# A fused decoder layer: how the row maxima are spread, a chain of loops written out, transposes for the maxima's row, and a rearranged end of the experts' part

## The chip, the cores and the metric

The kernel runs on one core of a Trainium2 chip. TensorE (PE in the profile) multiplies matrices, with PEld as its weight loads; VectorE is DVE, ScalarE is ACT, GpSimd is POOL, SyncE is SP. The metric is the device time of one launch in microseconds (us), the median of the runs.

## The reference

One decoder layer over 1024 tokens of width 128, in three parts, each followed by a layer norm: a Mamba2 pair (forward and backward), attention of the 1024 tokens to a context of 6404 rows plus the tokens themselves (8 heads of 128), and a mixture of 8 experts (each token goes to 2) with a shared expert. Cut to what the change touches:

```python
# attention: q from the layer's rows x, keys and values from [context, x]
sim = einsum('bhid,bhjd->bhij', q * DH ** -0.5, k)
out = einsum('bhij,bhjd->bhid', softmax(sim, axis=-1), v)     # then @ Wo + bo, residual, layer norm
# experts
topv, topi = top_k(softmax(xn @ router_w), 2); topv = topv / sum(topv)
out = sum over e of comb[:, e] * (silu(clip(gate_e, -10, 10)) * up_e) @ down_w[e]
out = out + shared expert
y = layernorm(x + out)
```

## The kernel before

**Attention** is 16 blocks (`NBLK`) of 512 query columns. A block runs through the keys in `NS` = 30 steps of two chunks of 128 keys: 7 head steps, a loop of 3 turns of 6 steps (`LOOP0`, `LOOPN`), 5 tail steps from `TAIL`. All operands are pairs of fp16 numbers (high and low part), so a chunk takes three products with A (scores) and three with the weights P (values), each 512 columns wide. In a step PE computes the scores, ACT takes the exponential twice (L1030 to fp16, L1033 to fp32), DVE subtracts for the low part (L1470), and PE multiplies with the values two steps later.

Meanwhile block b-1 finds the maxima of block b: 60 **units**, one PE product each into one of two banks of PSUM, read by a DVE maximum (L1438). PE may compute unit n only when unit n-2 has been read. `UNITS_HEAD` and `UNITS_TURN` say how many units stand in each step; three units stand in a step as one behind the first chunk's scores, one behind the second's, one between the two halves of the values; two units leave out the middle one. In its order DVE does a step's maxima first and then its low part. At the tail `max_to_row` turns the four columns of maxima into a row, DVE puts it into A (`max_row`), `project` multiplies the block before with the output matrix, and `a_side` computes A of the block after the next. From block 6 on `a_side` works by tile: 24 products of 128 columns, where before it takes 6 of 512. Blocks 0, 14 and 15 are written out; PE runs blocks 1 to 5, 6 to 8 and 9 to 13 in three loops with a register for the block's number.

Block 15 finishes tile 7 of the tokens (`LAST_TILE`). Tiles 0 to 6 (`FRONT`) are normalised, routed and sent to their slots during block 15.

**Experts** are 31 units of work in the order `ORDER`: 21 slots of 128 rows (13 of them with the expert's number in a register), the two halves of the shared expert, 8 experts on tile 7. For a unit PE computes gate and up, DVE clips the gate (`clip`, L1758), ACT takes silu (L1107), DVE multiplies (`hidden`, L1767), ACT casts to the high part (L1114), POOL or DVE subtracts the low part (L814, L1781), and PE multiplies down three units later. DVE runs `side_work` between them: norm, transposition and routing of tile 7. At the end the slots' rows come back from DRAM (`yt`), two per token, DVE adds them to `acc`, and the last norm goes to `xf` and by eight stores of one tile to the output.

The order of all work on an engine is the order of its code; between engines stand semaphores. A chain of norm pieces (`tile_norm`) waits after nearly every instruction (`settle`). The inverse root is computed with shifts and three Newton steps in it (L1510 to L1517).

## Time and profile before

| | us |
|---|---|
| median of 3 runs | 1765.81 (1763.61 to 1766.6) |
| the profiled execution's own time | 1766.59 |
| its span, first to last instruction | 1764.8 |
| PE busy | 1698.3 (96%) |
| DVE busy | 1450.4 (82%) |
| ACT busy | 1087.9 (62%) |
| POOL busy | 272.3 (15%) |

The profile is of one execution. A PE product's record is longer than the distance to the next one, since products overlap: the start times tell how fast they follow each other. The attention blocks lie between about 171 and 1665 us, the experts between 1666 and 1750 us, the last norm and the stores behind that.

### The profile page before, as it was taken

What the parts mean: (1) busy time and instruction counts of PE and PEld (TensorE: products, weight loads), DVE (VectorE), ACT (ScalarE), POOL (GpSimd) and SP (SyncE); (2) the same over time, 40 slices, a digit from 0 to 9 for tenths busy, and PEclk for the clock granted to TensorE, in tenths of its full rate; (3) what the DMA queues carried; (4) which work ended last, traced back from release to release, by engine and by line L of the source; (5) the groups of instructions that cost most, each with busy time, mean ns of one, the idle gap of its engine ahead of it and who ended that gap; (6) DMA issues with size and microseconds to landing.
All of it is one profiled execution on the core that took longest, in us unless ns stands there. A gap on an engine that the chain in (4) does not pass through costs nothing.

```text
span 1764.8 us, 31344 instructions
## 1 busy us (share of the span) xinstructions
PE 1698.3 (96%) x9273; PEld 860.6 (49%) x9273; DVE 1450.4 (82%) x2318; ACT 1087.9 (62%) x1333; POOL 272.3 (15%) x356
## 2 busy tenths in 40 slices
PE   6978999999999999999999999999999999999996
PEld 4855444444444444444444444444444444444585
DVE  7958988888888879797878888888879797877667
ACT  4555666666666666666666666666666666567663
POOL 4745993000000000000000000000000000001363
PEclk8989999999999999999999999999999999999998
DMA  5001110000000000000000000000000000000101
GB/s 179 2 1 37 55 55 4 0 0 0 0 0 0 0 0 0 0 0 0 0 0 0 0 1 0 0 0 0 0 0 0 0 0 0 1 0 1 54 25 43
DMA packets 20669, 20.24 MB, mean 11 GB/s; under 512 B 6735, under 2 KB 18259, under 8 KB 20230
## 3 DMA queue, kind: packets, MB, share of 16 engines
q1 hardware_dynamic: 19494, 17.20, 3.2%
q0 software_dynamic: 1120, 2.31, 0.4%
q8 instruction: 34, 0.56, 0.1%
q14 instruction: 21, 0.17, 0.0%
HBM read 15.27 MB, written 4.23 MB: 11 GB/s over the span
## 4 chain that ended last, share of the span: by engine, by line
PE 88%; DVE 5%; issue 3%; ACT 2%; POOL 0%; DMA 0%; DVEq 0%; ACTq 0%; POOLq 0%
PE PS L1875 88%; ACT p_arena L1040 1%; DVE mxs L1438 1%; DVE mxs L1719 1%; ACT p_arena L1033 1%; DVE w_arena L1219 0%; DVE z_arena L1767 0%; DVE w_arena L1393 0%; DMA w_arena<-in_x 0%; ACT z_arena L876 0%; POOL p_arena L814 0%; DVE w_arena L1207 0%; DVE m_arena L1520 0%; DVE p_arena L1470 0%; DVE m_arena L1399 0%
## 5 line engine op out<-in xcount | busy, mean ns | idle before, releaser
L1030 ACT ACTIVATE p_arena<-PS 128x1024 f16<-128x1024 f32 (+1 forms) x480 | 484.4, 1009 | 523.5 <-PE PS L1875 523.3
L1875 PE MATMUL PS<-a_arena,z_arena 128*128 (+1 forms) x2832 | 746.6, 380 | 1.5 <-DVE a_arena L1734 1.4
L1875 PE MATMUL PS<-p_arena,z_arena 128*128 128x512 f16 x2800 | 740.6, 379 | 1.4 <-ACT p_arena L1040 0.3
L1470 DVE TENSOR_TENSOR p_arena<-p_arena 128x1024 f16<-128x1024 f32 (+1 forms) x480 | 574.2, 1196 | 100.5 <-ACT p_arena L1033 90.2
L1438 DVE TENSOR_REDUCE mxs<-PS 128x512 f32 (+1 forms) x900 | 581.8, 667 | 86.6 <-PE PS L1875 83.2
L1033 ACT ACTIVATE p_arena<-PS 128x1024 f32<-128x1024 f32 (+1 forms) x480 | 482.0, 1004 | 0.0
L1875 PEld LDWEIGHTS PS<-a_arena,z_arena 128*128 (+1 forms) x2832 | 274.1, 98 | 326.8 <-issue 2.0
L1875 PEld LDWEIGHTS PS<-p_arena,z_arena 128*128 128x128 f16 (+1 forms) x2800 | 269.3, 98 | 311.8 <-ACT p_arena L1040 8.8
L1875 PE MATMUL PS<-z_arena,a_arena 128*128 (+3 forms) x1024 | 353.4, 360 | 10.4 <-DVE mxs L1438 8.1
L785 POOL IOTA r_arena<- 128x16 f32 x1 | 0.1, 145 | 1296.4 <-DVE acc L1484 1296.4
L1875 PEld LDWEIGHTS PS<-z_arena,a_arena 128*128 (+1 forms) x1024 | 97.8, 98 | 143.7 <-DVE mxs L1438 26.2
L1875 PE MATMUL PS<-w_arena 128*128 128x64 f32 (+5 forms) x268 | 40.3, 293 | 6.6 <-DVE w_arena L1219 3.9
L1719 DVE TENSOR_REDUCE mxs<-PS 128x2 f32<-128x1024 f32 (+1 forms) x30 | 34.1, 1184 | 10.9 <-PE PS L1875 10.8
L712 POOL TENSOR_SCALAR p_arena<-p_arena,mv,rs 128x127 f32<-128x127 f32 x50 | 41.8, 847 | 0.0
L1875 PE MATMUL PS<-z_arena,w_arena 128*128 128x128 f16 x504 | 37.9, 221 | 2.9 <-DVE z_arena L1767 1.6
L774 POOL TENSOR_SCALAR w_arena<-w_arena 128x256 f32<-128x256 f32 (+1 forms) x50 | 40.3, 806 | 0.0
L1758 DVE TENSOR_SCALAR z_arena<-PS 128x512 f32<-128x512 f32 x31 | 21.4, 690 | 23.0 <-PE PS L1875 16.1
L778 POOL TENSOR_TENSOR w_arena<-w_arena 128x256 f16<-128x256 f32 (+1 forms) x50 | 37.7, 754 | 4.2
L1875 PEld LDWEIGHTS PS<-VO,p_arena 128*128 128x128 f32 x256 | 33.4, 191 | 4.3
L1107 ACT ACTIVATE z_arena<-z_arena 128x512 f32<-128x512 f32 x31 | 19.5, 630 | 25.9 <-DVE z_arena L1758 25.9
L1875 PEld LDWEIGHTS PS<-z_arena,w_arena 128*128 (+1 forms) x504 | 31.6, 97 | 7.4 <-issue 3.3
L1020 ACT ACTIVATE a_arena<-PS 128x512 f32 (+1 forms) x32 | 19.1, 597 | 25.8 <-PE PS L1875 25.7
(323 smaller groups left out, 1019.4 us busy)
## 6 DMA issues: line engine op xcount, KB each, us to landing
w_arena<-in_L_ffn_gate_up_w SPq DMA_DIRECT2D x8, 512.0 KB, 3.6
p_arena<-in_ctx SPq DMA_DIRECT2D x2, 1600.0 KB, 9.1
w_arena<-in_L_ffn_down_w SPq DMA_DIRECT2D x8, 256.0 KB, 3.9
a_arena<-in_L_xattn_Wkv SPq DMA_DIRECT2D x1, 1024.0 KB, 5.7
a_arena<-xg_dram SPq DMA_DIRECT2D x12, 65.0 KB, 2.0
xg_dram<-VO SPq DMA_DIRECT2D x1, 715.0 KB, 7.4
xg_dram<-VO SPq DMA_DIRECT2D x1, 650.0 KB, 8.9
w_arena<-in_x SPq DMA_DIRECT2D x1, 512.0 KB, 4.3
```

Of the source, the lines that this page charges most:

```text
L712: g.tensor_scalar(ctx_sb[:, c, 1:P], ctx_sb[:, c, 1:P], mv[:, c, 0:1], rs[:, 3, c:c + 1], ALU.subtract, ALU.mult).then_inc(z_scaled, 1)
L774: g.tensor_scalar(src, src, WS, 0.0, ALU.mult, ALU.add).then_inc(w_scaled, 1)
L778: g.tensor_tensor(lo, src, hi, ALU.subtract).then_inc(stage_used, 1)
L1020: s.activation(A[:, b % 4, 2 * g, :], PS[:, 7 - g, :], ACT.Copy, scale=1 / AHS).then_inc(a_hi, 1)
L1030: s.activation(Phi[:, r % 3, 0:w], ps, ACT.Exp, scale=1 / SSC).then_inc(hi_ready, 1)
L1033: s.activation(P32[:, r % 2, 0:w], ps, ACT.Exp, scale=1 / SSC).then_inc(p32_ready, 1)
L1107: s.activation(sil[:, u % RING], gcl[:, u % RING], ACT.Silu, scale=1 / (XS * WS)).then_inc(f_silu, 1)
L1438: v.tensor_reduce(mxs[:, i, bass.ds(kb, 1)], PS[:, 6 + par, 0:w], AX.X, ALU.max).then_inc(mx_read, 1)
L1470: v.tensor_tensor(Plo[:, r % 3, at:w], P32[:, r % 2, at:w], Phi[:, r % 3, at:w], ALU.subtract).then_inc(lo_ready, 1)
L1719: v.tensor_reduce(mxs[:, i:i + 2, kb:kb + 1], PS[:, pair % 2 * 2:pair % 2 * 2 + 2, 0:w], AX.X, ALU.max).then_inc(mx_read, 2)
L1758: v.tensor_scalar(gcl[:, u % RING], PS[:, u % 2], lim, -lim, ALU.min, ALU.max).then_inc(f_clip, 1)
L1875: return t.matmul(o, l, r, start=start, stop=stop)
```

## The change

1. `UNITS_TURN` goes from 3, 3, 3, 3, 2, 2 to 2, 3, 3, 3, 3, 2 units per step of a loop turn.
2. `max_to_row` uses four transposes where four fp32 products with the identity stood.
3. PE's blocks 6 to 13 are written out, each with its numbers as constants; the loop over the turns inside a block stays.
4. Behind block 15 the evacuation `U_sb` is split between ACT and DVE, and the clip of unit 0 stands ahead of `project_acc`. PE waits for one semaphore more.
5. The norm of tile 7 goes one piece per unit, from unit 2 to 8 (`NORM0`), its transposition from step 5 to 10, its routing from step 10 to 15.
6. At the end POOL adds the slots' rows of tiles 0 to 3 and DVE those of tiles 4 to 6, ahead of the last low part; one chain of roots serves all 8 tiles; DVE writes rows of tiles 7 to 2, POOL of 0 and 1; three stores (tiles 5 to 7, 0 to 1, 2 to 4).

```diff
-UNITS_TURN = [3, 3, 3, 3, 2, 2]
+UNITS_TURN = [2, 3, 3, 3, 3, 2]
...
+NORM0, TURNED, ROUTED = 2, 10, 15
...
-    put(5, 1, "turned", 1, 0)
-    put(10, 1, "routed", 1, 0)
+    put(TURNED, 1, "turned", 1, 0)
+    put(ROUTED, 1, "routed", 1, 0)
...
-            for c in range(TC):
-                sp.wait_ge(fin, c + 1)
-                sp.dma_start(outr[:, c, :], xf[:, c, :]).then_inc(stored, 16)
-            sp.wait_ge(stored, 16 * TC)
+            sp.wait_ge(fin, 3)
+            sp.dma_start(outr[:, 5:TC, :], xf[:, 5:TC, :]).then_inc(stored, 16)
+            sp.wait_ge(base_rows, TC + 2)
+            sp.dma_start(outr[:, 0:2, :], xf[:, 0:2, :]).then_inc(stored, 16)
+            sp.wait_ge(fin, 6)
+            sp.dma_start(outr[:, 2:5, :], xf[:, 2:5, :]).then_inc(stored, 16)
+            sp.wait_ge(stored, 48)
...
+            def rows_added(part):
+
+                r = Y_TILES[part]
+                rows = acc[:, r.start:r.stop]
+                pool.wait_ge(yt_ld[part], 16)
+                for k in range(2):
+                    g.tensor_tensor(rows, rows, yt[:, r.start:r.stop, k], ALU.add).then_inc(half_acc, 1)
+                    pool.wait_ge(half_acc, k + 1)
...
+            pool.wait_ge(dn_acc, BY_DVE[number("shared", 1, NF - 1 - HT)])
+            rows_added(0)
+            pool.wait_ge(out_roots, 1)
+            for t in range(2):
+                norm_rows(xf[:, t, :], acc[:, t, :], t, t).then_inc(base_rows, 1)
...
-            evac(NBLK - 1)
+            act.wait_ge(pv_done, NS * NBLK)
+            act.wait_ge(o_ps, 2 * (NBLK - 1))
+            s.copy(U_sb[:, 0], PS[:, 4, :]).then_inc(u_evac, 1)
...
+            dve.wait_ge(pv_done, NS * NBLK)
+            v.tensor_copy(U_sb[:, 1], PS[:, 5, :]).then_inc(o_half, 1)
+            clip(0)
...
+            def front_added():
+
+                r = Y_TILES[1]
+                rows = acc[:, r.start:r.stop]
+                dve.wait_ge(dn_acc, BY_DVE[number("shared", 1, NF - 1 - HT)])
+                dve.wait_ge(yt_ld[1], 16)
+                for k in range(2):
+                    settle(v.tensor_tensor(rows, rows, yt[:, r.start:r.stop, k], ALU.add))
+
+            def out_stats(tiles):
+
+                for t in tiles:
+                    last = v.bn_stats(st6[:, t, :], acc[:, t, :])
+                return last
...
-                if u == 0:
-                    dve.wait_ge(o_acc, 2 * NBLK)
-                    tile_norm([LAST_TILE], 2 * NF, 0)
-                    tile_norm([LAST_TILE], 2 * NF, 1)
-                elif u in (1, 2):
-                    tile_norm([LAST_TILE], 2 * NF, 2 * u)
-                    tile_norm([LAST_TILE], 2 * NF, 2 * u + 1)
-                elif u == 3:
-                    tile_norm([LAST_TILE], 2 * NF, 6)
-                elif u == 7:
+                if NORM0 <= u < NORM0 + 7:
+                    if u == NORM0:
+                        dve.wait_ge(o_acc, 2 * NBLK)
+                    tile_norm([LAST_TILE], 2 * NF, u - NORM0)
...
             for u in range(NUNITS):
-                clip(u)
                 if u:
+                    clip(u)
...
             hidden(LAST_UNIT)
+            front_added()
             low_dve(LAST_UNIT)
             for u in range(NUNITS, NUNITS + 6):
                 for kind, a, t in work_at(u - 1, 0) + work_at(u - 1, 1):
                     small_dve(kind, a, t)
-            front_done(0)
-            front_done(1)
-            front_done(2)
-            front_done(3)
+            out_stats(Y_TILES[1])
+            dve.wait_ge(half_acc, 2)
+            out_stats(Y_TILES[0])
             dve.wait_ge(dn_acc, BY_DVE[-1])
             dve.wait_ge(last_ps, 1)
             added(LAST_TILE, LAST_BANK, cb[:, E - 1:E]).then_inc(dn_acc, 1)
             dve.wait_ge(dn_acc, BY_DVE[-1] + 1)
-            for piece in range(4, 9):
-                front_done(piece)
-            tile_norm([LAST_TILE], 2 * NF, 0, twice=False)
-            tile_norm([LAST_TILE], 2 * NF, 1, twice=False)
-            for piece in range(2, 7):
-                tile_norm([LAST_TILE], 2 * NF, piece, twice=False)
+            settle(out_stats([LAST_TILE]))
+            for piece in range(1, 6):
+                tile_norm(range(TC), 0, piece, twice=False)
+            dve.wait_ge(out_roots, 1)
+            for t in OUT_ROWS:
+                out_row(t, t).then_inc(fin, 1)
...
-                    last = mm(PS[0:1, row_bank(b), i * P:(i + 1) * P], mcol[:, 1, i:i + 1], I32[:])
+                    last = t.transpose(PS[0:1, row_bank(b), i * P:(i + 1) * P], mcol[:, 1, i:i + 1], I32[:])
...
-            with pe.Fori(H - 2, H + 1) as j:
-                block_pe(j, a_by_tile=True)
-            with pe.Fori(H + 1, NBLK - 2) as j:
-                block_pe(j, a_by_tile=True, by_tile=True)
+            for j in range(H - 2, NBLK - 2):
+                block_pe(j, a_by_tile=True, by_tile=j > H)
...
+                    pe.wait_ge(o_half, 2 * (NBLK - 1 - H) + 1)
```

How the change moves instructions, at three places. In these rows a name in brackets is the semaphore waited for.

On PE, the end of a block from 9 to 13, from the last values products ahead of `a_side` (`ah_arena` holds its left operand) on. Before:

```order
L1875 MATMUL PS<-p_arena,z_arena 128x512
L2366 REGISTER_ALU
L1875 ISA [waits o_acc]
L1875 ISA
L1875 MATMUL PS<-z_arena,ah_arena 128x128
L1875 ISA
L1875 MATMUL PS<-z_arena,ah_arena 128x128
```

and now:

```order
L1897 MATMUL PS<-p_arena,z_arena 128x512
L1897 MATMUL PS<-z_arena,ah_arena 128x128 [waits o_acc]
L1897 MATMUL PS<-z_arena,ah_arena 128x128 x23
L1897 MATMUL PS<-a_arena,z_arena 128x512 [waits p32_ready]
L1897 MATMUL PS<-a_arena,z_arena 128x512 x5
```

The 24 products stood among instructions that form their addresses in registers, one at each one or two products; now they stand alone.

On DVE, the first units of the experts (`gcl`, `sil` and `hid` lie in `z_arena`; L1758 is a clip, L1767 a `hidden`). Before:

```order
L1750 TENSOR_TENSOR a_arena<-a_arena,r_arena 128x21 [waits dve_step]
L1758 TENSOR_SCALAR z_arena<-PS 128x512 [waits f_gate]
L1499 BN_STATS st<-acc 128x6 [waits o_acc]
L1503 BN_AGGR mv<-st 128x2 [waits dve_step]
L1505 TENSOR_SCALAR rs<-mv 128x1 [waits dve_step]
L1507 TENSOR_SCALAR rs<-mv 128x1
L1758 TENSOR_SCALAR z_arena<-PS 128x512 [waits f_gate,dve_step]
L1767 SCALAR_TENSOR_TENSOR z_arena<-PS,z_arena 128x512 [waits f_up,f_silu]
```

and now (L1745 is the clip, L1795 `hidden`):

```order
L1778 COPY p_arena<-PS 128x512 [waits pv_done]
L1745 TENSOR_SCALAR z_arena<-PS 128x512 [waits f_gate]
L1498 RECIPROCAL rden<-PS 128x2 [waits o_ps]
L1505 SCALAR_TENSOR_TENSOR acc<-PS,rden,acc 128x128 [waits o_rd]
L1505 SCALAR_TENSOR_TENSOR acc<-PS,rden,acc 128x128 [waits o_half]
```

The clip of unit 0 passed `project_acc` and the slots' destinations, and the norm's pieces stand behind unit 1's `hidden`.

On DVE, the end, behind the last two `hidden`. Before:

```order
L1781 TENSOR_TENSOR p_arena<-z_arena,p_arena 128x512 [waits dn_ps,f_hi]
L1772 SCALAR_TENSOR_TENSOR acc<-PS,wt_arena,acc 128x128 [waits dn_acc,dn_ps] x3
L1814 TENSOR_TENSOR acc<-acc,z_arena 128x512 [waits yt_ld0,dn_acc]
L1816 TENSOR_TENSOR acc<-acc,z_arena 128x512 [waits half_acc]
L1814 TENSOR_TENSOR acc<-acc,z_arena 128x384 [waits yt_ld1]
L1816 TENSOR_TENSOR acc<-acc,z_arena 128x384 [waits half_acc]
L1499 BN_STATS st<-acc 128x6 [waits half_acc]
```

and now:

```order
L1841 TENSOR_TENSOR acc<-acc,z_arena 128x384 [waits yt_ld1,dn_acc]
L1841 TENSOR_TENSOR acc<-acc,z_arena 128x384 [waits dve_step]
L1809 TENSOR_TENSOR p_arena<-z_arena,p_arena 128x512 [waits dn_ps,f_hi,dve_step]
L1800 SCALAR_TENSOR_TENSOR acc<-PS,wt_arena,acc 128x128 [waits dn_acc,dn_ps] x3
L1846 BN_STATS st<-acc 128x6 x3
L1846 BN_STATS st<-acc 128x6 [waits half_acc]
```

Two adds went to POOL (waited for by `half_acc`), the other two passed the last low part.

## Rows read from the trace of the kernel before

**Rows 1.** Busy time by stretch: start:end, length, each engine's busy time, PEclk, DMA

```profile
642.50:736.10 93.60, 93.08 (x447) 43.17 (x446) 79.23 (x106) 59.38 (x65) 0.00 (x0) 1.00 0.00 0
1020.40:1115.20 94.80, 94.20 (x465) 44.23 (x464) 79.42 (x106) 59.38 (x65) 0.00 (x0) 1.00 0.00 1
1494.50:1586.70 92.20, 91.69 (x438) 42.47 (x437) 77.33 (x106) 58.21 (x63) 1.85 (x14) 1.00 0.00 1
1586.70:1663.00 76.30, 75.95 (x390) 37.62 (x388) 54.13 (x131) 55.05 (x60) 23.61 (x21) 1.00 0.07 19
```

**Rows 2.** Timeline of block 13's tail on PE: start, length, engine, line, operation

```profile
1471.43 1.46 PE L1875 MATMUL PS<-p_arena,z_arena 128*128 128x512 f16 x6
1472.73 1.46 PE L1875 MATMUL PS<-a_arena,z_arena 128*128 x6
1474.12 1.03 PE L1875 MATMUL PS<-I,mcol 128*1 128x128 f32 x8
1475.08 1.47 PE L1875 MATMUL PS<-p_arena,z_arena 128*128 128x512 f16 x6
```

**Rows 3.** Timeline of PE in block 15, seven fp32 transposes

```profile
1595.74 0.94 PE L2225 MATMUL PS<-I,m_arena 128*128 128x128 f32 x7
1596.51 1.46 PE L1875 MATMUL PS<-a_arena,z_arena 128*128 128x512 f16 x6
```

**Rows 4.** Timeline of PE around `a_side` of block 13, then in the experts

```profile
1482.06 1.46 PE L1875 MATMUL PS<-p_arena,z_arena 128*128 128x512 f16 x6
1483.60 2.35 PE L1875 MATMUL PS<-z_arena,ah_arena 128*128 x24
1485.84 1.47 PE L1875 MATMUL PS<-a_arena,z_arena 128*128 x6
...
1739.14 1.50 PE L1875 MATMUL PS<-wt_arena,w_arena 128*128 128x128 f16 x24
1740.48 0.83 PE L1875 MATMUL PS<-w_arena,p_arena 128*128 128x128 f16 x12
```

**Rows 5.** Timeline of block 13's first turn; brackets: idle before, releaser

```profile
1414.27 1.03 PE L1875 MATMUL PS<-p_arena,z_arena 128*128 128x512 f16 x4
1415.00 1.97 DVE L1438 TENSOR_REDUCE mxs<-PS 128x512 f32 x3
1415.74 0.39 PE L1875 MATMUL PS<-z_arena,a_arena 128*128 x1 [0.44 <-DVE mxs L1438]
```

**Rows 6.** DMA of instructions over the span: packets, MB, share

```profile
q8 instruction: 34, 0.56, 0.1%
```

**Rows 7.** Timeline of PE in the first units of the experts

```profile
1671.29 0.83 PE L1875 MATMUL PS<-z_arena,w_arena 128*128 128x128 f16 x12 [0.48 <-DVE z_arena L1758]
1673.19 1.59 PE L1875 MATMUL PS<-z_arena,w_arena 128*128 128x128 f16 x24 [1.07 <-DVE z_arena L1767]
1676.51 1.09 PE L1875 MATMUL PS<-z_arena,w_arena 128*128 128x128 f16 x12 [0.58 <-DVE z_arena L1767]
```

**Rows 8.** Timeline of POOL and DVE there, then DVE's small steps at the end

```profile
1673.87 1.16 POOL L814 TENSOR_TENSOR p_arena<-z_arena,p_arena 128x512 f16<-128x512 f32 x1 [16.78 <-ACT p_arena L1114]
1673.91 1.13 DVE L1517 SCALAR_TENSOR_TENSOR wt_arena<-rs,wt_arena 128x2 f32<-128x2 f32 x1
...
1757.22 0.17 DVE L1514 TENSOR_TENSOR rs<-wt_arena 128x7 f32<-128x7 f32 x1
```

**Rows 9.** Timeline of DVE at the end, and the stores (count, KB each, us to landing)

```profile
1750.35 0.68 DVE L1814 TENSOR_TENSOR acc<-acc,z_arena 128x512 f32<-128x512 f32 x1
1752.85 1.45 DVE L1499 BATCH_NORM_STATS2 st<-acc 128x6 f32<-128x128 f32 x7
1757.83 1.88 DVE L1520 TENSOR_SCALAR m_arena<-acc,mv,rs 128x128 f32<-128x128 f32 x7
1762.53 0.34 DVE L1520 TENSOR_SCALAR m_arena<-acc,mv,rs 128x128 f32<-128x128 f32 x1
out<-m_arena SPq DMA_DIRECT2D x8, 64.0 KB, 1.6
```

More of the change, by code:

```diff
@@ L577, in layer @@
         LAST_BANK = LAST_UNIT % 2
+        OUT_ROWS = range(TC - 1, 1, -1)
         Y_TILES = [range(0, 4), range(4, NF)]
@@ L814, in _ @@
                     g.tensor_tensor(lo, hid[:, u % RING], hi, ALU.subtract).then_inc(f_lo, 1)
-                if u == 5:
+                if u == TURNED:
                     pool.wait_ge(xf_ready, 2)
@@ L1143, in _ @@
                         rows_turned_act(k)
-                if u == 6:
+                if u == TURNED + 1:
                     half_act(1, 0)
-                elif u == 15:
+                elif u == ROUTED + 5:
                     half_act(1, 1)
@@ L1482, in project_acc @@
                         last.then_inc(o_half, 1)
-                        dve.wait_ge(o_half, 2 * (b - H) + k + 1)
+                        dve.wait_ge(o_half, 2 * (b - H) + k + (2 if isinstance(b, int) and b == NBLK - 1 else 1))
                     last = v.scalar_tensor_tensor(out=acc[:, t, :], in0=o[:, i, 0:D], scalar=rden[:, 2 * k + i:2 * k + i + 1],
@@ L1488, in _, with out_row @@
             MAGIC = float(0x5F3759DF)
+            def out_row(t, at):
+                return v.tensor_scalar(xf[:, t, :], acc[:, t, :], mv[:, t, 0:1], rs[:, 3, at:at + 1], ALU.subtract, ALU.mult)
             def tile_norm(tiles, at, piece, twice=True):
@@ L1516, in tile_norm @@
                     dst = rs[:, 3, cols] if piece == 5 else y
-                    settle(v.scalar_tensor_tensor(out=dst, in0=rs[:, 1, cols], scalar=1.5, in1=y, op0=ALU.add, op1=ALU.mult))
+                    last = v.scalar_tensor_tensor(out=dst, in0=rs[:, 1, cols], scalar=1.5, in1=y, op0=ALU.add, op1=ALU.mult)
+                    if piece == 5 and not twice:
+                        last.then_inc(out_roots, 1)
+                    else:
+                        settle(last)
                 else:
                     for k, t in enumerate(tiles):
-                        last = v.tensor_scalar(xf[:, t, :], acc[:, t, :], mv[:, t, 0:1], rs[:, 3, at + w - n + k:at + w - n + k + 1],
-                                               ALU.subtract, ALU.mult)
-                        if not twice:
-                            last.then_inc(fin, 1)
-                    if twice:
-                        last.then_inc(xf_ready, 1)
+                        last = out_row(t, at + w - n + k)
+                    last.then_inc(xf_ready, 1)
             def turned(cols, bank):
@@ L1712, in block_dve, with clip @@
                         a_low(j + 2)
+            def clip(u):
+                dve.wait_ge(f_gate, u + 1)
+                if u >= RING:
+                    dve.wait_ge(f_silu, u + 1 - RING)
+                lim = 10.0 * XS * WS
+                v.tensor_scalar(gcl[:, u % RING], PS[:, u % 2], lim, -lim, ALU.min, ALU.max).then_inc(f_clip, 1)
             for pair in range(NU // 2):
@@ L1750, in _ @@
             v.tensor_tensor(posd, xg_f[:, :, D], unused, ALU.add).then_inc(dest_ready, 1)
-            def clip(u):
-                dve.wait_ge(f_gate, u + 1)
-                if u >= RING:
-                    dve.wait_ge(f_silu, u + 1 - RING)
-                lim = 10.0 * XS * WS
-                v.tensor_scalar(gcl[:, u % RING], PS[:, u % 2], lim, -lim, ALU.min, ALU.max).then_inc(f_clip, 1)
             def hidden(u):
@@ L1804, in small_dve @@
                     v.memset(ui[:, 0:1], 0.0).then_inc(dn_acc, 1)
-            def front_done(piece):
-                if piece < 2:
-                    if piece == 0:
-                        dve.wait_ge(dn_acc, BY_DVE[number("shared", 1, NF - 1 - HT)])
-                    r = Y_TILES[piece]
-                    dve.wait_ge(yt_ld[piece], 16)
-                    rows = acc[:, r.start:r.stop]
-                    v.tensor_tensor(rows, rows, yt[:, r.start:r.stop, 0], ALU.add).then_inc(half_acc, 1)
-                    dve.wait_ge(half_acc, 2 * piece + 1)
-                    v.tensor_tensor(rows, rows, yt[:, r.start:r.stop, 1], ALU.add).then_inc(half_acc, 1)
-                else:
-                    if piece == 2:
-                        dve.wait_ge(half_acc, 4)
-                    tile_norm(FRONT, 0, piece - 2, twice=False)
@@ L1834, in side_work @@
+            def out_stats(tiles):
+                for t in tiles:
+                    last = v.bn_stats(st6[:, t, :], acc[:, t, :])
+                return last
+            def side_work(u):
+                if NORM0 <= u < NORM0 + 7:
+                    if u == NORM0:
+                        dve.wait_ge(o_acc, 2 * NBLK)
+                    tile_norm([LAST_TILE], 2 * NF, u - NORM0)
+                elif u == TURNED + 2:
                     turned_low(1)
-                elif 12 <= u < 15:
-                    route(1, u - 12)
-                elif 17 <= u < 21:
-                    route(1, u - 14)
+                elif ROUTED + 2 <= u < ROUTED + 5:
+                    route(1, u - ROUTED - 2)
+                elif ROUTED + 7 <= u < ROUTED + 11:
+                    route(1, u - ROUTED - 4)
```

2 lines of the change are left out of this document (1 added, 1 removed).

## The prediction, made before the changed kernel had run

> **What bounds the kernel now.** I read busy time by stretch first, then the timeline of one attention block, then that of the last 100 us. In an attention block PE is the bound: 94.20 of 94.80 us busy at a granted clock of 1.00, with DVE at 79.42 and ACT at 59.38 [rows 1]. Products of 512 columns follow each other every 0.216 us: six start at 1471.43 and the next six at 1472.73, 1.30 us apart [rows 2]. So a microsecond less on PE in a block is a microsecond less in the time, unless DVE or ACT then comes late; DVE has 15 us of room per block. What is not 512 columns wide, or waits, is what the change can take. The experts are a chain through PE, DVE, ACT and POOL while it fills, then PE's. Behind 1750 us there is only DVE, in steps of 0.2 us, and the stores.
>
> **Maxima's row.** In `max_to_row` the four fp32 products (eight records) start at 1474.12 and the next ones at 1475.08: 0.96 us [rows 2]. Seven fp32 transposes of the same 128 columns take from 1595.74 to 1596.51, 0.77 us, so 0.11 each and 0.44 for four [rows 3]. Nothing covers them on PE: 0.52 less per block. Blocks 0 to 14 have maxima: 15 x 0.52 = 7.8 us. Bounds: the transposes of rows 3 load 128 columns of weights and these load one, so they may be quicker (all 0.96 gone: 14.4), or no quicker than now (0). I take the nearest row, 7.8. DVE's `max_row` is released 0.5 us sooner, which costs nothing.
>
> The row says 0.44 for four transposes. The Trainium skill, TensorE: Matmul & The Clock Gate, section Terms, calls the transpose mode four times faster for fp32; by that four would take 0.24 and the term would be 10.8. In its Part 4: PE-mode transpose it says that transposes do not count as PE-busy for the clock the way products do, which would speak against this edit; the stretch that holds the seven of rows 3 was at 1.00 throughout [rows 1].
>
> **Blocks written out.** In block 13 `a_side` comes behind six products from 1482.06, which are through at 1483.36; it starts at 1483.60 and lasts until 1485.84, together 2.48 us, or 0.093 per product [rows 4]. 24 products of the same shape with constant addresses, in the experts, take from 1739.14 to 1740.48: 1.34 us, 0.056 each [rows 4]. The difference is the address work in registers, an instruction at each one or two products. 1.14 us less, in blocks 6 to 13: 9.1 us. A second way to it: blocks with six wide products instead take 93.60 where these take 94.80 [rows 1], 1.2 us more, though 24 x 0.056 is about what six wide ones need. Bounds: 0, if the pace is that of weights of this operand; 10 if other address work in these blocks costs something too. I take 9.1. Against it stands the fetching of more code: instructions are 34 packets, 0.56 MB, in all [rows 6], and PE's code grows by half. Block 14 is already written out with the same loop inside, and takes 92.20 [rows 1], which is 94.80 less the `a_side` of 2.48 that it lacks (92.32). So written-out code as such costs nothing there.
>
> **Units per step.** In the first turn, first step, PE has four values products from 1414.27, through at 1415.13, and should compute the step's third unit. It starts at 1415.74: 0.61 us late, since DVE was still at the low part and began the step's first maximum only at 1415.00 [rows 5]. The step before is short (one chunk's values), so PE had run ahead of DVE there. With two units in that step the third does not stand there; PE goes on with the last two values products. In the next step, now of three, DVE has read one maximum fewer (1.97 / 3 = 0.66), and finds itself 0.66 earlier relative to PE, which is more than the 0.61 it was late. The three-unit steps are four in a row as before, and a turn still has 16, so the later steps repeat what they were. One place per block, 15 blocks: 9.1 us. Bounds: 0, if the stall only moves a step; below that, -3, if the three-unit step that now stands one place nearer the tail makes `max_column` late by 0.2. It has room there: the row's products start 0.09 us behind the scores, through at 1474.03, so they hardly wait [rows 2]. I take 9.1.
>
> **Start of the experts.** PE's idle spells ahead of the first products that wait for DVE add up to 0.48 + 1.07 + 0.58 = 2.13 us [rows 7]. They come from clip 0, which waits behind `project_acc`, and then from the pieces of tile 7's norm, one of which lasts 1.13 us instead of 0.16 [rows 8]. The clip of unit 0 now waits for its product alone, which takes the 0.48; the first `hidden` gains less, since unit 1's clip ahead of it stays behind the same `project_acc`. The norm's pieces are gone until unit 2. I take 2.0 of the 2.13. DVE's copy of half of `U_sb` lies beside ACT's and ends before PE asks. Bounds: 3.5, if the later units' shorter waits go too; -1, if pieces in units 4 to 8 meet POOL's low parts and hold up a clip or a low part. The later routing (steps 15 to 25) still ends ahead of the first dense unit's add, so I cost it at nothing; if it were late, the add waits on DVE with the next clips queued behind it.
>
> **The end.** DVE adds from 1750.35 to 1752.85 (2.50), writes the first row at 1757.83, seven rows in 1.88 (0.27 each), and then goes once more through everything for tile 7 until 1762.87; the store lands 1.6 later [rows 9]. Now: the adds leave this path (-2.5), tile 7's statistics join (+0.4, one row more in each of two steps). That gives roots at 1755.7. Against it: POOL and DVE get in each other's way. A DVE instruction of two columns with two operands in SBUF, started 0.04 behind a POOL pass of 1.16, lasted 1.13 and ended with it, where such a step takes 0.17 [rows 8]. DVE's two adds and the last low part have two operands in SBUF, and POOL's last low part and two adds of 512 run just then. Two such waits of 1 us: roots at 1757.7, about where they were. Six rows of 0.27 then end at 1759.3 instead of 1762.9. POOL's two rows, at most 1.16 each, end at 1760.0, and the third store waits for the second: issued at 1760.2 instead of 1762.9. That is 2.7 less; without the waits 4.7; with both adds and the low part each held up twice, 0.7. I take 2.7.
>
> The Trainium skill, SBUF — State Buffer, section Who interferes with whom, has the same as a lock: a DVE instruction with two SBUF inputs and a GpSimd one that reads SBUF exclude each other, whichever starts first. By that rule, the trace agrees.
>
> **The sum.** 7.8 + 9.1 + 9.1 + 2.0 + 2.7 = 30.7. The profiled execution took 1766.59 (its span is 1764.8, 1.8 less), so 1735.9; the median of the runs is 0.8 below it: 1735.
>
> **Rivals.** (a) The stall moves: the unit that waits is another one, and the change of `UNITS_TURN` gives nothing. For it: DVE is as full as before in three-unit steps, where 1.97 of PE's 15 x 0.216 = 3.24 go to the maxima and most of the rest to the low part [rows 2, 5]. Against it: the walk above. 1744. (b) `a_side` keeps its pace, for each product loads new weights. For it: its operand is another one than the experts'. Against it: same shape, same count at 0.056. 1744. (c) Transposes with one column of weights take 0.24: 1732. (d) Slower: code. Each written-out block enters its loop of turns at a new address, and if PE must wait there for its instructions, that comes once or more per block. From 3.8 us per block (30.7 / 8) it cancels all the rest; at 5 us per block the time is 1735 + 40 = 1775. For it: PE's code grows by half, and no row shows a long run of written-out blocks. Against it: block 14 [rows 1]. (e) The clock falls to its lower level of 1.2 GHz behind the transposes: one step of 2.6 us at half the pace in 15 blocks is 39 us more, 1774; against it the 1.00 of the stretch with seven of them.
>
> **Chances.** Forecast 0.70, with a range of its own of 1730 to 1741; (a) 0.10; (b) 0.07; (c) 0.05; (d) 0.03; (e) 0.01; the edits do next to nothing together 0.04. I count as no change what lies within 0.2% (3.5 us), about what a measurement of this kernel can tell. Faster: 0.70 + 0.10 + 0.07 + 0.05 = 0.92; same 0.03; slower 0.05, with (d), (e) and a quarter of the rest. The range reaches from (c) with a better end, 1728, to (a) or (b) with a worse start and end, 1748.
>
> **What would show it.** In the changed kernel's trace: four records of transposes with 0.44 us to the next product; the 24 products of `a_side` within 1.34 us and no gap ahead; no idle spell behind L1438 at the first step of a turn; blocks 6 to 13 at 92.5 us, blocks 1 to 5 at the same; PE's idle spells in the first 15 us of the experts under 1 us; DVE steps of over 1 us while POOL adds; the last row's end at 1759 less the 28 us gained ahead. Blocks that shrink by less than 1.5 us would make the prediction wrong, and a block with a new idle spell at its loop's entry would show (d).

## The result and the profile after

The changed kernel takes 1740.11 us (median of 4 runs, 1737.27 to 1740.54), the kernel before in the same comparison 1765.56 (4 runs): a ratio of 0.9853, 95% interval 0.984 to 0.9865, 25.5 us less. It is faster, and the time lies within the range and 5 us above the 1735 forecast. The profiled execution took 1739.8, its span 1737.8; before they were 1766.59 and 1764.8. The sum of the prediction said 30.7 less, the spans say 27.0. The sections below find the missing 3.7, which is what several larger misses leave when they are added up.

First the busy time by stretch, for the counterparts of [rows 1] (start:end, length, busy us and instructions of PE, PEld, DVE, ACT, POOL, then PEclk and the DMA's share and rate):

```profile
618.40:711.20 92.80, 92.72 (x444) 42.88 (x443) 78.95 (x107) 59.39 (x63) 0.00 (x0) 1.00 0.00 0
1082.60:1175.50 92.90, 92.82 (x462) 43.71 (x461) 79.19 (x107) 59.39 (x63) 0.00 (x0) 1.00 0.00 0
1564.40:1640.70 76.30, 75.95 (x390) 37.62 (x389) 54.18 (x131) 55.05 (x60) 23.62 (x21) 1.00 0.07 19
```

A block with wide `a_side` went from 93.60 to 92.8, one by tiles from 94.80 to 92.9; the prediction had 92.5 for both. The last block is as long as before. The granted clock is 1.00, the 2.4 GHz level, with four transposes in each block. PE's timeline in block 13, counterpart of [rows 2] and [rows 4] (start, length, engine, line, operation):

```profile
1453.03 1.46 PE L1897 MATMUL PS<-a_arena,z_arena 128*128 128x512 f16 x6
1454.32 0.60 PE L2224 MATMUL PS<-I,mcol 128*1 128x128 f32 x4
1454.76 1.46 PE L1897 MATMUL PS<-p_arena,z_arena 128*128 128x512 f16 x6
...
1461.73 1.46 PE L1897 MATMUL PS<-p_arena,z_arena 128*128 128x512 f16 x6
1463.02 1.50 PE L1897 MATMUL PS<-z_arena,ah_arena 128*128 128x128 f16 x24
1464.36 1.46 PE L1897 MATMUL PS<-a_arena,z_arena 128*128 128x512 f16 x6
```

The records of the 24 products of `a_side` span 1.50 where they spanned 2.35; the next product starts 1.34 after the first of them, and no gap stands ahead (1461.73 + 6 x 0.216 = 1463.02). Four transposes stand where eight records stood, and the next product starts 0.44 us behind them, as forecast. They also start 1.29 us behind the six scores, which is their pace; the eight records before started 1.39 behind [rows 2]. Then the place of [rows 5], in the changed kernel (brackets: idle before, and releaser):

```profile
1396.76 1.23 DVE L1491 TENSOR_TENSOR p_arena<-p_arena 128x1024 f16<-128x1024 f32 x1
1397.75 1.03 PE L1897 MATMUL PS<-p_arena,z_arena 128*128 128x512 f16 x4
1397.90 2.08 DVE L1459 TENSOR_REDUCE mxs<-PS 128x512 f32 x3
1398.76 0.39 PE L1897 MATMUL PS<-z_arena,a_arena 128*128 x1
...
1416.89 1.03 PE L1897 MATMUL PS<-p_arena,z_arena 128*128 128x512 f16 x4
1417.90 0.39 PE L1897 MATMUL PS<-z_arena,a_arena 128*128 x1
```

Four products of 0.216 from 1397.75 are through at 1398.61; the step's third unit starts at 1398.76. So the wait of 0.61 is gone, but this is the second step of the turn, and it now waits 0.15 us, in the first turn, in the second (1417.90 instead of 1417.75), and in the third. Instructions over DMA, for [rows 6]:

```profile
q8 instruction: 48, 0.79, 0.2%
```

14 packets more, and no idle spell at a block's entry. The experts' start, for [rows 7], with one later place, and the end, for [rows 9]:

```profile
1643.65 1.50 PE L1897 MATMUL PS<-z_arena,w_arena 128*128 128x128 f16 x24 [0.25 <-DVE z_arena L1649]
1649.55 1.71 PE L1897 MATMUL PS<-z_arena,w_arena 128*128 128x128 f16 x24 [0.32 <-DVE z_arena L1795]
1699.43 1.28 ACT L1070 ACT_TABLE_LOAD   x1
1700.95 1.28 ACT L1169 ACT_TABLE_LOAD   x1
1704.85 0.33 PE L1897 MATMUL PS<-w_arena,p_arena 128*128 128x128 f16 x3 [1.65 <-POOL p_arena L828]
```

```profile
1722.69 1.98 DVE L1841 TENSOR_TENSOR acc<-acc,z_arena 128x384 f32<-128x384 f32 x2
1722.90 1.35 POOL L828 TENSOR_TENSOR p_arena<-z_arena,p_arena 128x512 f16<-128x512 f32 x1 [1.42 <-ACT p_arena L1135]
1724.21 3.25 POOL L805 TENSOR_TENSOR acc<-acc,z_arena 128x512 f32<-128x512 f32 x2
1724.70 1.64 DVE L1809 TENSOR_TENSOR p_arena<-z_arena,p_arena 128x512 f16<-128x512 f32 x1
1727.44 1.44 DVE L1846 BATCH_NORM_STATS2 st<-acc 128x6 f32<-128x128 f32 x7
...
1732.66 1.68 DVE L1513 TENSOR_SCALAR m_arena<-acc,mv,rs 128x128 f32<-128x128 f32 x6
1732.81 1.81 POOL L810 TENSOR_SCALAR m_arena<-acc,mv,rs 128x128 f32<-128x128 f32 x2 [5.34 <-DVE rs L1542]
out<-m_arena SPq DMA_DIRECT2D x2, 192.0 KB, 2.0
```

The idle spells of 0.48, 1.07 and 0.58 are down to one of 0.32; in the first 17 us of the experts PE is idle only for 0.20, 0.12 and 0.14 besides. Behind the two table loads of the routing's exp PE waits 1.65. In the kernel before, PE did not wait there:

```profile
1710.36 1.28 ACT L1051 ACT_TABLE_LOAD   x1
1711.87 1.28 ACT L1148 ACT_TABLE_LOAD   x1
1714.13 0.83 PE L1875 MATMUL PS<-w_arena,p_arena 128*128 128x128 f16 x12
```

At the end DVE's low part takes 1.64 beside POOL's adds, and one root chain is followed by six rows on DVE and two on POOL, side by side. A store of 192 KB lands 2.0 us after its issue, one of 64 KB took 1.6.

### The profile page after: what moved, and what is told of

Its sections match the earlier page's. It is cut to its first block, busy times and chain, and to the rows that moved or that the text cites. A ratio compares the mean times of both kernels' runs of the same rounds, so it can differ in the third digit from the quotient of the medians.

```text
span 1737.8 us, 30711 instructions
## 1 busy us (share of the span) xinstructions
PE 1682.0 (97%) x9213; PEld 854.0 (49%) x9213; DVE 1444.2 (83%) x2302; ACT 1087.4 (63%) x1333; POOL 279.8 (16%) x360
## 4 chain that ended last, share of the span: by engine, by line
PE 90%; DVE 4%; ACT 3%; issue 2%; POOL 1%; DMA 0%; SPq 0%; POOLq 0%; ACTq 0%; DVEq 0%
PE PS L1897 89%; ACT p_arena L1059 1%; DVE mxs L1752 1%; ACT p_arena L1052 1%; POOL p_arena L828 0%; PE PS L2224 0%; DVE w_arena L1240 0%; DVE w_arena L1414 0%; ACT z_arena L895 0%; DVE z_arena L1795 0%; POOL w_arena L678 0%; DMA vecs<-in_L_attn_b_conv_w 0%; PE PS L1906 0%; ACT p_arena L1135 0%; SPq L449 0%
## 5 line engine op out<-in xcount | busy, mean ns | idle before, releaser
L1897 PE MATMUL PS<-a_arena,z_arena 128*128 128x512 f16 (+1 forms) x2832 | 746.8, 380 | 1.4 <-DVE a_arena L1767 1.4
L1897 PEld LDWEIGHTS PS<-z_arena,a_arena 128*128 128x128 f16 (+1 forms) x1024 | 98.2, 98 | 136.7 <-issue 22.1
L783 POOL TENSOR_TENSOR w_arena<-w_arena 128x256 f16<-128x256 f32 (+1 forms) x50 | 41.7, 834 | 4.2
L1745 DVE TENSOR_SCALAR z_arena<-PS 128x512 f32<-128x512 f32 x31 | 21.4, 690 | 19.8 <-PE PS L1897 14.6
L779 POOL TENSOR_SCALAR w_arena<-w_arena 128x256 f32<-128x256 f32 (+1 forms) x50 | 35.7, 714 | 0.0
L1897 PE MATMUL PS<-w_arena,p_arena 128*128 128x128 f16 (+1 forms) x372 | 29.7, 220 | 5.5 <-POOL p_arena L828 4.1
L1897 PEld LDWEIGHTS PS<-w_arena 128*128 128x128 f32 (+3 forms) x268 | 25.5, 141 | 18.9 <-issue 7.1
```

Source lines behind the costliest of these rows:

```text
L779: g.tensor_scalar(src, src, WS, 0.0, ALU.mult, ALU.add).then_inc(w_scaled, 1)
L783: g.tensor_tensor(lo, src, hi, ALU.subtract).then_inc(stage_used, 1)
L1745: v.tensor_scalar(gcl[:, u % RING], PS[:, u % 2], lim, -lim, ALU.min, ALU.max).then_inc(f_clip, 1)
L1897: return t.matmul(o, l, r, start=start, stop=stop)
```

## Experiments

All kernels were profiled as well. Where the loading phase ends differs by up to 3.5 us from one profile to the next, though no edit touches it (block 0's first scores start between 165.3 and 168.8), so terms of a few us are read inside the traces: block = distance between the loads of the maxima's row in successive blocks, experts = from unit 0's first product to unit 30's clip, end = from that clip to the span's end. All in us:

```
kernel                        blocks 2-6  blocks 7-14  experts   end    median
before                          93.61        94.80      79.37   19.57
before, transposes only         92.98        94.15      79.28   19.55   1754.03
before, written out only        93.61        93.66      79.76   19.56   1757.06
changed                         92.83        92.87      76.98   17.18   1740.11
changed, turn back              92.98        93.02      77.08   17.18   1740.84
changed, turn 2,2,3,3,3,3       92.37        92.41      76.92   17.19   1731.23
changed, turn 2,3,3,3,2,3       92.83        92.87      77.78   17.18
changed, turn 3,3,2,2,3,3       93.20        93.25      77.69   17.20
changed, DVE adds all           92.83        92.87      77.73   17.49   1739.29
changed, start back             92.83        92.87      80.43   17.19   1741.92
2,2,3,3,3,3 + copy split        92.12        92.16      78.12   17.18   1732.70
2,2,3,3,3,3 + low first, 13     92.37        92.41      76.99   18.65
2,2,3,3,3,3 + split, not in 15  92.12        92.16      77.99   17.18   1731.62
```

Blocks agree within 0.05 between profiles of the same code. The experts don't: 76.9 to 78.1, with nothing changed there. To see where the experts' part gains or loses, these are some of its clips, in us behind unit 0's first product:

```
kernel                     unit 15   unit 16   unit 22   unit 23   unit 30
before                      42.23     45.54     61.56     63.55     79.37
changed                     38.61     42.20     57.61     61.11     76.98
changed, turn 2,3,3,3,2,3   38.61     42.85     58.18     61.66     77.78
changed, start back         42.70     45.57     62.63     64.62     80.43
```

**Transposes alone**, on the kernel before.

```diff
-                    last = mm(PS[0:1, row_bank(b), i * P:(i + 1) * P], mcol[:, 1, i:i + 1], I32[:])
+                    last = t.transpose(PS[0:1, row_bank(b), i * P:(i + 1) * P], mcol[:, 1, i:i + 1], I32[:])
```

> The kernel before with nothing but the transposes in max_to_row. Theory of the prediction's term: 0.52 us less in each of 15 blocks, 7.8 us, so 0.9956 of the time before, 1757.8, and blocks 1 to 5 at 93.1 instead of 93.6. Rival (the 0.6 us of the next place that waits eats part of it, since DVE is the later one in the first turn): 0 to 4 us less, with blocks of 93.4 to 93.6.

Measured: 0.9943, interval 0.9928 to 0.9957, and 93.61 - 92.98 = 0.63 less in a block, 0.11 more than the term. (The median is 12.0 us lower, where 15 x 0.63 is 9.5: in the profiled execution the first scores also start 3.0 sooner, at 165.8 instead of 168.8.) PE's timeline around one row:

```profile
616.24 1.46 PE L1875 MATMUL PS<-a_arena,z_arena 128*128 x6
617.54 0.60 PE L2202 MATMUL PS<-I,mcol 128*1 128x128 f32 x4
617.97 0.81 PE L1875 MATMUL PS<-p_arena,z_arena 128*128 128x512 f16 x3
```

From the scores to the transposes it is 6 x 0.216 = 1.30: no gap. Before there was 0.09 to 0.10 [rows 2]. The weights' loader shows what it was (kernel before, same place):

```profile
1472.51 1.18 PEld L1875 LDWEIGHTS PS<-a_arena,z_arena 128*128 128x128 f16 x6
1474.12 0.74 PEld L1875 LDWEIGHTS PS<-I,mcol 128*1 128x1 f32 x8 [0.42 <-issue]
```

The first load of this fp32 product isn't done ahead, beside the last score, but starts with the product at 1474.12; that of the transposes (1454.11 for 1454.32 in the changed kernel) is. It was not a wait for the maxima: DVE had finished them 1.76 us before. Nor is it so for every fp32 product: `project`'s, with weights of 128 columns instead of one, load at 1477.47 for 1477.68 in the same block. So the 0.10 belonged to the products of this place and went with them; why their load comes late stays open. The rival fell: nothing was eaten.

**Blocks written out alone**, on the kernel before.

```diff
-            with pe.Fori(H - 2, H + 1) as j:
-                block_pe(j, a_by_tile=True)
-            with pe.Fori(H + 1, NBLK - 2) as j:
-                block_pe(j, a_by_tile=True, by_tile=True)
+            for j in range(H - 2, NBLK - 2):
+                block_pe(j, a_by_tile=True, by_tile=j > H)
```

> The kernel before with nothing but PE's blocks 6 to 13 written out. Theory of the prediction's term: 1.14 us less in each of 8 blocks, 9.1 us, so 0.9948 of the time before, 1756.7, and a_side's 24 products within 1.34 us. Rival (written-out code costs something at the loops of turns it enters, which the shorter a_side hides in the changed kernel): less than 8 us gained.

Measured: 0.9947, interval 0.9933 to 0.996, 9 us, and 94.80 - 93.66 = 1.14 in each of 8 blocks, to the hundredth the term. The rival fell.

**The turn.** Four lists of 16 units, all on the changed kernel; the edit is `UNITS_TURN` alone. First as before the change, [3, 3, 3, 3, 2, 2]:

> The changed kernel with UNITS_TURN back at [3, 3, 3, 3, 2, 2]; all else as changed. Theory 1 (the rotation took the 0.61 us stall of a block's first turn but made three of 0.15 us, one in each turn's second step): a block is longer by 0.61 - 0.44 = 0.17 us than in the changed kernel, up to 0.27 by the blocks 1 to 5 of the two traces; with block 0, 3 to 5 us more, 1743 to 1745. The trace has PE late by 0.61 in the first step of the first turn and nowhere else in the turns. Theory 2 (the prediction's: the whole 0.61 was gained and the shortfall of the blocks comes from elsewhere): 9 us more, 1749.

Measured: 0.9865, interval 0.985 to 0.988. The block grows by 0.15 us and no more, so the rotation was worth 2.3 us in 15 blocks instead of 9.1. Theory 1 stands by the blocks, though its 1743 to 1745 was too high; theory 2 fell. The one stall of 0.61 is in the trace again:

```profile
650.61 1.03 PE L1897 MATMUL PS<-p_arena,z_arena 128*128 128x512 f16 x4
651.33 1.28 DVE L1459 TENSOR_REDUCE mxs<-PS 128x512 f32 x2
652.07 0.39 PE L1897 MATMUL PS<-z_arena,a_arena 128*128 x1 [0.43 <-DVE mxs L1459]
```

Then both short steps at the start, [2, 2, 3, 3, 3, 3]:

> The changed kernel with UNITS_TURN = [2, 2, 3, 3, 3, 3]: both two-unit steps stand at the start of a turn. Theory 1 (the third unit of a turn's second step is late by 0.15 us since the low part ahead of it waits for ACT, whose passes of a turn's first step start 0.09 us later than those of other steps): the first step of three is now the third one, its low part ahead hangs on no turn's start, and the three places of 0.15 go: 0.44 per block, 15 blocks, 6.6 us less than the changed kernel: 1733.5. Theory 2 (every first three-unit step behind two-unit ones is late by 0.15 us, wherever it stands): the same time as the changed kernel, 1740. Theory 3 (a three-unit step as the last one before the tail makes the column's maxima late): 1741 to 1743, with PE idle ahead of the transposes of the maxima's row.

Measured: 0.9812, interval 0.9799 to 0.9826, 8.9 us below the changed kernel's median; by the blocks 0.46 each, 6.9 in 15. A three-unit step ahead of the tail costs nothing. Which step waits was right; the reason was not yet shown, so two lists more:

> The changed kernel with UNITS_TURN = [2, 3, 3, 3, 2, 3]. Theory 1 (PE's third unit of a step comes early where two-unit steps stand ahead, by 0.22 us for each, and the low part ahead of it hangs on ACT, late by 0.09 where a turn starts): in the first turn two two-unit steps are ahead of the first three-unit one as now, 0.15 late; in turns two and three only one is, so nothing there; the second three-unit step behind a single two-unit one doesn't wait either. Blocks of 92.37 + 0.15 = 92.52 us instead of 92.83. Theory 2 (the second step of a turn always costs 0.15): blocks of 92.8.

Measured: one run, 1743.22, blocks of 92.83: as with [2, 3, 3, 3, 3, 2], so the number of short steps ahead doesn't matter and the expected 92.52 was wrong. The second turn of a block shows why:

```profile
674.35 1.02 ACT L1052 ACTIVATE p_arena<-PS 128x1024 f32<-128x1024 f32 x1
675.40 1.23 DVE L1491 TENSOR_TENSOR p_arena<-p_arena 128x1024 f16<-128x1024 f32 x1 [0.17 <-ACT p_arena L1052]
676.39 1.03 PE L1897 MATMUL PS<-p_arena,z_arena 128*128 128x512 f16 x4
676.54 2.08 DVE L1459 TENSOR_REDUCE mxs<-PS 128x512 f32 x3
677.39 0.10 PEld L1897 LDWEIGHTS PS<-z_arena,a_arena 128*128 x1 [0.47 <-issue]
```

DVE's low part waits for ACT, and ACT for PE's scores: behind a short step the chain hangs on PE itself, whatever lead PE has. And the load of the third unit starts at 677.39 although the maximum it waits for was over at 676.54 + 0.68 = 677.22; a load that had to wait for a maximum starts 0.05 behind it elsewhere (652.06 for 652.01 in the stall above). What stands between is in the program's order for PE, at the third unit of the second step:

```
1565 L2207 REGISTER_ALU
1566 L1897 ISA [waits mx_read]
1567 L1897 MATMUL PS<-z_arena,a_arena 128x512
```

The units of a turn take their columns by fours, and at unit 4 a new address is put in a register. The wait stands on that instruction, and the product comes behind it. [3, 3, 2, 2, 3, 3] puts unit 12, of the same kind, third in a step behind a short one, away from the turn's start:

> The changed kernel with UNITS_TURN = [3, 3, 2, 2, 3, 3]. The units of a turn go by fours through ZThi, and PE loads a new address register at units 0, 4, 8 and 12; the semaphore's wait of such a unit stands on that register instruction, the product behind it. Theory R (a third unit that comes just in time is late where it is one of these four: it was unit 4 in the second step with [2, 3, 3, 3, 3, 2] and [2, 3, 3, 3, 2, 3], units 2 and 6 where nothing was late): here the third unit of the fifth step, behind two two-unit steps, is unit 12, so that place is late by 0.11 to 0.15 in each turn, and the first step of the first turn by 0.61 as before the change: blocks of 92.37 + 0.61 + 0.33 to 0.45 = 93.3 to 93.4 us. Theory T (what is late hangs on the start of the turn): only the 0.61 of the first turn, blocks of 92.98.

Measured: one run, 1743.88, blocks of 93.20, 0.22 above those of [3, 3, 3, 3, 2, 2]. PE in the first turn:

```profile
664.79 1.03 PE L1897 MATMUL PS<-p_arena,z_arena 128*128 128x512 f16 x4
665.72 0.39 PE L1897 MATMUL PS<-z_arena,a_arena 128*128 x1
```

0.07 late (665.65 would be in time), and so in each turn. Theory R holds in kind, and is half of the size. The maximum was over at 665.55 and the load starts 0.16 behind it, at 665.71, as in the two lists before; so the register ahead of the product costs 0.11, of which 0.04 is slack here. Here the maximum ends 0.10 ahead of the values products, with [2, 3, 3, 3, 3, 2] only 0.02 (655.66 and 655.68), and so nothing of the 0.11 is slack there. These 0.08 fit what ACT shows: where the step before is a turn's first, its first pass starts 0.93 behind the second group of scores (672.50 to 673.43 with [2, 3, 3, 3, 2, 3]), elsewhere 0.85 (1429.99 to 1430.84 in the kernel before). This part is read, not tested by itself.

**The copy of `U_sb`.** With [2, 2, 3, 3, 3, 3] the only stall left in a block is PE's wait of 0.24 for ACT's copy in step 2.

```diff
-                s.copy(U_sb, PS[:, 4:6, :]).then_inc(u_evac, 1)
+                s.copy(U_sb[:, 0], PS[:, 4, :]).then_inc(u_evac, 1)
...
+                    if st == 1 and not first:
+                        dve.wait_ge(pv_done, NS * j)
+                        v.tensor_copy(U_sb[:, 1], PS[:, 5, :]).then_inc(u_evac, 1)
                     low(j, st)
```

> The kernel with UNITS_TURN = [2, 2, 3, 3, 3, 3], and U_sb copied by two engines in every block: ACT copies the bank of one half (0.6 us instead of 1.02) and DVE the other, ahead of the low part of step 1, where the trace has DVE idle for 0.56 us. Theory 1 (the last stall of a block is PE's wait for ACT's copy in step 2, 0.24 us): 0.24 less in 15 places, 3.6 us less than with the same turn and ACT's copy alone: 1731.2 - 3.6 = 1727.6, blocks of 92.13. Rival (DVE's copy makes its low part late by 0.2 us or more, and what follows waits for it: ACT's next pass, then PE): the same time or up to 3 us more, 1731 to 1734.

Measured: 0.9803, interval 0.979 to 0.9817. Blocks of 92.12 as expected, but from the last maxima's row to unit 0's first product it took 98.80 instead of 96.65: over half of the gain was given back. (The experts also took 1.2 longer, but they do so in other runs without the split.) Without the split in block 15, where DVE also does tiles' norms:

> The kernel with UNITS_TURN = [2, 2, 3, 3, 3, 3] and the copy of U_sb split between ACT and DVE in blocks 1 to 14, but not in block 15, where the split one was late (DVE also does the norm there, and PE lost 2.0 us). Theory (the 0.25 us per block that the split gave stays, the 2.0 are not lost): 0.25 x 14 = 3.4 us less than with the turn alone, blocks of 92.12 and 1227 us less than nothing else changed: 1731.2 - 3.4 = 1727.8. Rival (the loss in block 15 was the run's and not the split's): the same blocks, but a last part as long as in the split kernel, 98.8 us from the last transposes to unit 0's first product instead of 96.65, 1730.

(The words on 1227 us in it are a slip.) Measured: 0.9798, interval 0.9784 to 0.9813. The last part is back at 96.66, blocks at 92.12: the theory holds for these. The experts took 77.99, in the upper half of what they vary by, and of the expected 3.4 us the medians show little; the interval overlaps that of the turn alone. This kernel, or the turn alone, is 8 to 9 us faster than the changed one by the medians, and 7 to 10 by the ratios.

**The end: DVE adds all.**

```diff
-            rows_added(0)
...
-                r = Y_TILES[1]
+                for part, r in enumerate(Y_TILES):
```

> The changed kernel with DVE alone adding the routed experts' rows at the end, as before the change (POOL adds none); the rest of the tail as changed. What POOL takes off DVE is one part's adds, 2.50 - 1.3 = 1.2 us; what it costs DVE is the hold-ups: in the trace DVE's adds took 1.98 instead of 1.3, its low part 1.64 instead of 1.23, 1.1 us together. Theory 1 (the two cancel since POOL and DVE exclude each other on two SBUF operands): within 0.5 us of the changed kernel, 22.7 us from the clip of unit 30 to the end less what noise there is. Rival (the hold-ups are DVE's waits for something else and stay): 1.2 to 1.5 us more.

Measured: 0.9851, interval 0.9838 to 0.9865; the end 17.49 instead of 17.18. Theory 1 stands: POOL's share of the adds is worth 0.31 us.

```profile
1721.83 3.42 DVE L1839 TENSOR_TENSOR acc<-acc,z_arena 128x512 f32<-128x512 f32 x4
1722.04 1.48 POOL L828 TENSOR_TENSOR p_arena<-z_arena,p_arena 128x512 f16<-128x512 f32 x1 [1.41 <-ACT p_arena L1133]
1725.29 0.69 DVE L1807 TENSOR_TENSOR p_arena<-z_arena,p_arena 128x512 f16<-128x512 f32 x1
```

DVE's low part takes 0.69 with POOL idle and 1.64 beside POOL's adds: that 0.95 pays for most of what POOL takes over. (The 1.23 in the expectation was for a pass of twice the width.)

**The start of the experts back.**

```diff
-            clip(0)
...
-                if NORM0 <= u < NORM0 + 7:
+                if u == 0:
```

> The changed kernel with the start of the experts as before the change: clip 0 behind project_acc, the pieces of tile 7's norm from unit 0 on (two in a step), its transposes at step 5, its routing from step 10 on; the copy of U_sb by two engines stays. Theory (the prediction's term): 2.0 us more, up to 2.4 by the two traces between unit 0's first product and clip 30; PE idle 0.5, 1.1 and 0.6 us ahead of the second units as before. Rival (the later routing and the copy made the gain, or the shift of 2.4 came from elsewhere in the experts): within 0.5 us of the changed kernel.

Measured: 0.9856, interval 0.9841 to 0.9871; the experts 80.43 instead of 76.98, 3.4 more, of which up to 1.2 may be their own variation.

```profile
1650.09 0.83 PE L1901 MATMUL PS<-z_arena,w_arena 128*128 128x128 f16 x12 [0.48 <-DVE z_arena L1745]
1651.99 1.59 PE L1901 MATMUL PS<-z_arena,w_arena 128*128 128x128 f16 x24 [1.07 <-DVE z_arena L1794]
1655.31 1.11 PE L1901 MATMUL PS<-z_arena,w_arena 128*128 128x128 f16 x12 [0.58 <-DVE z_arena L1794]
```

The same idle spells as in [rows 7] are back, at the same places. The medians alone, 1.8 us apart with overlapping intervals, wouldn't show it. That the start made the gain stands, its size does not: by unit 15's clip this kernel is 4.1 us behind the changed one and the kernel before 3.6, not 2.0 to 2.4. Behind it the changed kernel loses some of that again, with PE's wait of 1.65 at the table loads, which this one doesn't have. The edit puts start, transposition and routing back together, so the routing's share is read from the clips, not tested by itself.

**Low part ahead of the adds, routing at step 13**, on [2, 2, 3, 3, 3, 3].

```diff
-            front_added()
             low_dve(LAST_UNIT)
+            front_added()
```

> The kernel with UNITS_TURN = [2, 2, 3, 3, 3, 3] and two edits in different stretches, each read from its own. First, the routing of the last tile at steps 13 to 24 instead of 15 to 26: from unit 0's first product to unit 30's clip it took 76.9 to 77.1 us, of which PE waits 1.65 at the step behind the two table loads of the routing's exp; if the place of the loads decides, this changes by up to 0.8, otherwise it stays within 0.3. Second, DVE's last low part ahead of its two adds: from unit 30's clip to the end it took 17.16. Theory 1 (DVE is busy throughout there and the hold-ups by POOL are what the order can change): 16.5 to 17.0. Rival (DVE now waits for ACT's last pass before the low part, about 0.8 us that the adds filled): 17.5 to 18.0.

Measured: one run, 1735.44. The experts 76.99, so steps 13 and 15 come to the same. The wait of 1.65 is gone and PE waits at most 0.81 at one place, but unit 15's clip comes at 38.81 and unit 22's at 58.76 where [2, 2, 3, 3, 3, 3] alone has 38.62 and 57.56: what was saved at one place was lost at others. The end 18.65, 1.5 more: the rival holds, and costs more than it said.

```profile
1717.88 1.15 DVE L1809 TENSOR_TENSOR p_arena<-z_arena,p_arena 128x512 f16<-128x512 f32 x1 [0.68 <-ACT p_arena L1135]
1718.43 3.26 POOL L805 TENSOR_TENSOR acc<-acc,z_arena 128x512 f32<-128x512 f32 x2
1718.95 3.16 DVE L1841 TENSOR_TENSOR acc<-acc,z_arena 128x384 f32<-128x384 f32 x2
```

DVE stood idle for 0.68, and then its adds met POOL's: 3.16 instead of 1.98.

## Why the prediction was right in the time and wrong in a term

```
term               forecast   measured
maxima's row          7.8        9.5    0.63 x 15
blocks written out    9.1        9.1    1.14 x 8
units per step        9.1        2.3    0.15 x 15
start of experts      2.0        2.4    79.37 - 76.98
the end               2.7        2.4    19.57 - 17.18
sum                  30.7       25.7    spans: 27.0
```

Of the 1.3 that the spans have beyond the sum, 1.0 to 1.1 are block 0 and the loading ahead of it, which differ by more than that between profiles of one code, and 0.3 lies between the last maxima's row and the experts.

**Maxima's row.** The transposes take the 0.44 taken from [rows 3]. The term was too small because the 0.09 ahead of the products was read as a wait that stays ("they hardly wait"), where it was these products' own late load of weights. Rival (c), 0.24 for four, did not come, nor did (e): the four in each block ran at a granted clock of 1.00. So the factor of four that the Trainium skill gives in TensorE: Matmul & The Clock Gate, section Terms, does not show: 0.96 to 0.44 is 2.2, or 2.4 with the 0.10 ahead.

**Blocks written out.** Right in mechanism and size, to 0.01 us per block. (The prediction's 0.093 per product leaves out the gap of 0.24 ahead; 2.48 / 24 is 0.103.) Rival (b), the pace of the weights, and rival (d), code, are out: 14 packets of instructions more, no idle spell.

**Units per step** is the step that failed. "The later steps repeat what they were" doesn't hold: the list repeats as a ring, but the turn has a start of its own. The three-unit step that follows the short ones moved from a turn's first place to its second, where its third unit is unit 4. A maximum that came just in time in turns two and three (before, PE's third unit came without delay at 1434.74) became a wait of 0.15 in all three turns, 0.11 of it from the address register of unit 4, ahead of which PE waits. The prediction counted what DVE gains in the first turn, 0.66 against 0.61, and asked of no other turn which instruction the wait stands on. Rival (a), "the stall moves", was three quarters true, at 0.10. The difference to the forecast is 6.8 us, and the larger row term and the rest give back 2.

**Start of the experts.** 2.4 for 2.0 looks right and is partly luck, for two misses cancel. By unit 15's clip the changed kernel has gained 3.6 us (42.23 to 38.61), with the same products done on PE but for two small ones of the router, above the 2.13 of idle spells that the prediction counted and even above its bound of 3.5. Of this, 1.2 is gone at unit 30: between the clips of units 22 and 23, where PE waits 1.65 behind the routing's table loads, it takes 3.50 instead of 1.99. The prediction put the later routing at nothing; in the kernel before, routed from step 10, PE has no such wait. Whether the new start with the routing left at step 10 would keep the 3.6, no run shows. And since the experts' part varies by up to 1.2 between profiles of one code, the 2.4 could have come out anywhere from 1.2 to 2.8; the 3.6 is firm to 0.3, for at unit 15 the profiles with the new start agree within 0.02 (0.2 with the routing at step 13) and those with the old start of the kernel before within 0.28.

**The end.** Roots were forecast at 1757.7 in the time of before; they end at 1732.65, which with the 24.64 that unit 30's clip has moved (1745.27 to 1720.63) is 1757.3. DVE's last row is through at 1734.34 + 24.64 = 1759.0, POOL's at 1759.3 (forecast 1759.3 and 1760.0). The lock between POOL and DVE was seen twice, as assumed, and makes POOL's adds worth 0.31 us. What the term gains is the one chain of roots and the shared rows. The last store is issued at 1735.07 + 24.64 = 1759.7 instead of 1762.9, 3.2 sooner where 2.7 was forecast; being larger, it lands 2.08 later instead of 1.53, and from its landing to the span's end it is 0.66 instead of 0.41, which takes 0.8 back.

## What to carry to other kernels

Where a wait is just met, moving work to another place of a loop needs the same question at every turn of the loop: what does the step hang on there, and on which instruction does its wait stand; an address register loaded behind the wait costs 0.11 us each time, less what slack there is. Read small terms inside a trace, between two marks that nothing else moves, since here the load phase alone varied by 3 us; and set a mark in the middle too, for a term that comes out right at its end may be a gain of 3.6 and a loss of 1.2. Two engines that exclude each other on SBUF operands share work for almost nothing: 1.2 us of adds given away saved 0.31.

## What the runs showed that was not expected

The fp32 products with one column of weights leave a gap of 0.10 us ahead of them, as their first load does not go beside the product before; transposes of the same operand leave none, nor do fp32 products with 128 columns of weights. A semaphore's wait on a register instruction ahead of a product costs 0.11 us over the same wait on the product (the load starts 0.16 instead of 0.05 behind the maximum). And the experts' part takes 76.9 to 77.1 or 77.7 to 78.1 us with the same instructions, at a granted clock of 1.00 in both. The two groups part at one place: unit 16's clip comes 3.5 to 3.6 us behind unit 15's in the first and 4.2 in the second; what decides stays open.
